# The last, short chunk of tokens goes through all experts densely instead of by scatter and gather

## The reference

```
x = h.reshape(T, D)                                  # T = 16 * 3137 tokens, D = 64
probs = softmax(x @ gate_w + gate_b); idx = argmax(probs); prb = probs[idx]
pos = (cumsum(one_hot) * one_hot).sum(-1) - 1        # place of the token in its expert's list
kept = pos < C                                       # C = ceil(1.25 * T / 8)
buf[idx, pos] = x
hmid = relu(buf @ w1 + b1)                           # 64 -> 256
ybuf = hmid @ w2 + b2                                # 256 -> 64
y_tok = ybuf[idx, min(pos, C - 1)] * (prb * kept)
h = h + y
```

## Time and profile before

| | |
|---|---|
| time, median of 3 runs | 4353.44 us (4352.43 to 4363.89) |
| the profiled execution's own time | 4361.58 us |
| its span, first to last instruction | 4359.7 us |
| PE busy | 3178.4 us (73%) |
| DVE busy | 2525.0 us (58%) |
| POOL busy | 2575.4 us (59%) |
| ACT busy | 2138.1 us (49%) |
| granted TensorE clock, mean | 0.863 of full |

### The profile page before, as it was taken

One profiled execution on the slowest core, in us unless ns is written; L12 is line 12 of the kernel. 1 busy time (PEld: TensorE's weight loads), 2 busy tenths in 40 slices (PEclk: granted clock), 3 DMA queues, 4 the chain that ended last, 5 costly groups with the idle time before them and its releaser, 6 DMA issues. The chain is left out here.

```text
span 4359.7 us, 68616 instructions
## 1 busy us (share of the span) xinstructions
PE 3178.4 (73%) x25552; PEld 1804.6 (41%) x25552; DVE 2525.0 (58%) x3049; ACT 2138.1 (49%) x3049; POOL 2575.4 (59%) x1541
## 2 busy tenths in 40 slices
PE   8999996999999940000099946676666899999997
PEld 6777774455555520000044312222221455555556
DVE  7888886888888851000055513333237777777772
ACT  6666665777777720000034335565552444444444
POOL 7777773878778716777600065555516666666661
PEclk9999998999999965555599967778777999999999
DMA  1111111122222121111133323333330111112111
GB/s 42 38 40 40 40 40 56 58 73 86 68 75 79 46 68 38 40 45 35 23 106 112 103 59 94 91 99 100 88 100 21 41 55 52 52 50 59 53 47 41
DMA packets 252194, 267.20 MB, mean 61 GB/s; under 512 B 86568, under 2 KB 168140, under 8 KB 251805
## 3 DMA queue, kind: packets, MB, share of 16 engines
q1 hardware_dynamic: 215566, 228.51, 16.8%
q0 software_dynamic: 25600, 21.10, 2.7%
q10 hardware_dynamic: 10704, 13.20, 0.9%
HBM read 127.66 MB, written 140.20 MB: 61 GB/s over the span
## 5 line engine op out<-in xcount | busy, mean ns | idle before, releaser
L1512 POOL DMA_INDIRECT D_row<-yb,D_idx x400 | 385.1, 963 | 635.8 <-DMA D_prob<-keepp 346.9
L2150 POOL TENSOR_TENSOR E_w<-E_w,E_rs 128x1024 f32<-128x1024 f32 x200 | 380.4, 1902 | 365.0 <-DVE E_rs L2073 365.0
L1241 POOL DMA_INDIRECT xb<-R_row,R_si x400 | 389.7, 974 | 212.2 <-issue 121.6
L1314 PE MATMUL X_px<-X_ident,X_xs 128*128 128x128 f32 x256 | 42.9, 291 | 559.6 <-DMA X_xs<-xb 559.6
L180 POOL TENSOR_TENSOR A_kmask<-A_ksb,A_pack_a 128x3584 f32<-128x3584 f32 x56 | 356.6, 6367 | 152.6 <-ACT A_ksb L327 152.6
L1373 ACT ACTIVATE X_hm<-X_ph,X_b 128x512 f32<-128x512 f32 x128 | 88.1, 688 | 595.6 <-PE X_ph L1326 595.6
L2058 DVE TENSOR_REDUCE E_mx<-E_lg 128x16 f32<-128x1024 f32 x200 | 244.9, 1224 | 219.6 <-PE E_lg L1867 219.3
L1388 DVE COPY X_xt<-X_px 128x512 f32<-128x512 f32 x64 | 43.6, 681 | 531.1 <-PE X_px L1314 531.1
L2144 POOL TENSOR_TENSOR E_hs<-E_w 128x512 f32<-128x512 f32 x200 | 255.1, 1275 | 93.4 <-ACT E_w L2031 93.4
L1879 PE MATMUL E_z<-E_w,E_yk 128*64 128x512 f32 (+1 forms) x800 | 224.5, 634 | 78.1 <-POOL E_w L2150 76.9
L1314 PEld LDWEIGHTS X_px<-X_ident,X_xs 128*128 128x128 f32 x256 | 27.5, 143 | 608.2 <-DMA X_b<-in_e_b 559.7
(11 more groups left out here) (292 smaller groups left out, 8394.0 us busy)
## 6 DMA issues: line engine op xcount, KB each, us to landing
xb<-B_blank SPq DMA_DIRECT2D x64, 256.0 KB, 3.9
X_xs<-xb SPq DMA_DIRECT2D x64, 256.0 KB, 2.8
yb<-X_ys SPq DMA_DIRECT2D x64, 256.0 KB, 2.0
B_x<-h SPq DMA_DIRECT2D x25, 512.0 KB, 4.2
h<-B_hh SPq DMA_DIRECT2D x25, 512.0 KB, 3.7
y<-B_yt SPq DMA_DIRECT2D x25, 512.0 KB, 2.6
R_row<-y SPq DMA_DIRECT2D x25, 512.0 KB, 3.3
A_xg<-in_xw SPq DMA_DIRECT2D x56, 224.0 KB
```

The costliest lines, as they stand in the source:

```text
L1241: pool.indirect_dma_start(out=xb, out_offset=bass.IndirectOffsetOnAxis(ap=si[:, B * c + b:B * c + b + 1], axis=0), in_=row[c % U][:, D * r ...
L1512: pool.indirect_dma_start(out=row[n % LR][:, k, b], out_offset=None, in_=yb, in_offset=bass.IndirectOffsetOnAxis(ap=idx[:, c, i:i + 1], ax ...
L2150: TT(w3, w3, bc(rs[g % 3][:].unsqueeze(2), [128, 2 * SH, G]), ALU.mult).then_inc(w_done, 1)
```

## The change

The last chunk leaves the scatter and the gather. Its 16 x 65 real tokens go through all eight experts in stage R, while POOL scatters the other 24 chunks. Two images lie on the two partition halves, and four pairs are side by side, so that a block has 4 x 65 = 260 columns; there are NB = 2 blocks and so 16 steps (block, expert). At each step the tokens of other experts are zeroed by a mask, and what eight experts make of a zero (their biases) is taken out again by a constant per chosen expert (`cbt`). All experts are added up in one PSUM accumulator, the sum is scaled by the probability and added to h1 in DRAM.

Stage D reads that sum from h1 for its narrow blocks and skips `weigh`, `turn_rows` and `add_experts` there. The narrow block's loaded buffer is read until `add_hidden`, and `load` waits for that.

The row buffers of R go from 6 to 4. The weights of X come in one packed transfer of 3418 values per partition, which R loads as well. Stage R has 26 more semaphores for the dense part and 4 fewer for the row buffers.

```diff
-def routing(nc, a, lg, y2, xb, gidx, keepp):
+def routing(nc, a, lg, y2, xb, gidx, keepp, h1):
-        N, U = CHUNKS * B, 6
+        N, U = CHUNKS * B, 4
...
                 sp.dma_start(flat(L)..., lg...).then_inc(loads_in, 16)
+                sp.dma_start(pack[:], a["pack_x"]).then_inc(w_in, 16)
+                sp.dma_start(pick[:], a["c_pick"]).then_inc(w_in, 16)
+                sp.dma_start(held[:], y2[LAST]).then_inc(held_in, 16)
...
# PE, beside the scatter
+                def mask(s):
+                    i, e = divmod(s, E)
+                    pe.wait_ge(ohc_done, i + 1)
+                    after(pe, xe_done, s - 1)
+                    mm(ob[s % 2], pick[:, 2 * D * e:2 * D * e + 2 * D], oht[i % 2], start=True, stop=True)...
+                def up(s):
+                    pe.wait_ge(xe_done, s + 1)
+                    for f in range(2):
...
+                        for b in range(2):
+                            last = mm(ph[b][f], w1[HALF[b], s % E, 128 * f:128 * f + 128], xe[s % 3][HALF[b], :], ...)
+                def down(s):
+                    for f in range(2):
...
+                        for b in range(2):
+                            last = mm(acc[HALF[b], :], w2[:, s % E, f], hm[s % 2][:, b, f], start=False, ...)
...
# DVE, before the scatter starts
                 TT(X[:], L[:], by(mx), ALU.subtract).then_inc(sub_done, 1)
+                dve.wait_ge(w_in, 32)
+                TS(rb1[:], part["b1"]..., 0.0, None, ALU.max).then_inc(rb_done, 1)
+                dve.wait_ge(rb_done, 1)
+                for f in range(2):
+                    last = TT(r8[:, :, f], ...)
                 dve.wait_ge(totc_done, len(cuts))
...
# DVE, beside the scatter
+                def masked(s):
...
+                    TT(xe[s % 3], ob[s % 2], xt[i % 2], ALU.mult).then_inc(xe_done, 1)
+                def relu(s, f, b):
...
+                    TS(hm[s % 2][:, b, f], ph[b][f], part["b1"][:, k:k + 1], 0.0, ALU.add, ALU.max)...
+                def final(i):
...
+                    TT(xo[i % 2], px, yt[i % 2], ALU.mult).then_inc(t_done, 1)
...
+                    TT(xo[i % 2], xo[i % 2], hx[i % 3], ALU.add).then_inc(xo_done, 1)
...
# POOL
-                for c in range(CHUNKS):
+                for c in range(LAST):
...
 def experts(nc, a, xb, yb):
-                    spread(nc, sp, loads[:-1], consts)
+                sp.dma_start(pack[:], a["pack_x"]).then_inc(consts, 16)
...
 def image_recurrence(...):
+        Z = PAIRS * (J - 1)
+        def sparse(n):
+            return n % J != J - 1
+        def before(n):
+            if n >= N:
+                return Z
+            return n // J * (J - 1) + n % J
...
                 def load(n):
-                    after(sp, x_done, n - LH + 1)
+                    if n >= LH:
+                        if sparse(n - LH):
+                            sp.wait_ge(x_done, before(n - LH) + 1)
+                        else:
+                            sp.wait_ge(h_done, n - LH + 1)
...
-                for n in range(N):
-                    after(pool, sc_done, n - LR + 1)
+                for z in range(Z):
+                    after(pool, sc_done, z - LR + 1)
+                    n = block_of(z)
...
                 def turn_rows(n):
+                    if not sparse(n):
+                        return
...
                 def center_in(n):
-                    pe.wait_ge(x_done, n + 1)
+                    token_ready(pe, n)
...
                 def turn_y(n):
                     pe.wait_ge(yo_done, n + 1)
-                    after(pe, x_done, min(n + 5, N))
+                    after(pe, x_done, before(n + 5))
+                    after(pe, yk_done, n)
...
                 def weigh(n):
+                    if not sparse(n):
+                        return
...
                 def add_experts(n):
+                    if not sparse(n):
+                        return
```

More of the change, by code:

```diff
@@ L25 @@
 BLK = 512
+DENSE_PAIRS = 4
 CAPP = -(-CAP // BLK) * BLK
@@ L43 @@
     "f": (("ident", 128), ("bo", 1)),
+    "x": (("w1", E * F), ("w2", 2 * E * D), ("b1", 2 * E), ("b2t", E), ("ident", 128), ("other", 2 * E * E), ("b2r", D),
+          ("half", 2)),
 }
@@ new lines, in _, with turn_x @@
+                pe.wait_ge(w_in, 32)
+                pe.wait_ge(r8_done, 1)
+                for e in range(E):
+                    for f in range(2):
+                        last = mm(acc[0:2 * E, 0:D], r8[:, e, f], w2[:, e, f], start=e + f == 0, stop=e + f == E)
+                last.then_inc(c_done, 1)
+                pe.wait_ge(totc_done, len(cuts))
+                pe.wait_ge(prb_done, 1)
+                def turn_x(i):
+                    pe.wait_ge(held_in, 16)
+                    after(pe, t_done, i - 1)
+                    for k in range(BT):
+                        for b in range(2):
+                            r = D * row_of(2 * (BT * i + k) + b)
+                            last = mm(px[HALF[b], tokens(k)], held[0:TAIL, r:r + D], ident[0:TAIL, 0:TAIL],
+                                      start=True, stop=True)
+                    last.then_inc(turn_done, 1)
@@ new lines, in turn_oh @@
+                def turn_oh(i):
+                    pe.wait_ge(xtc_done, i + 1)
+                    for k in range(BT):
+                        last = turn(px[0:2 * E, tokens(k)], oh[0:TAIL, images(i, k)].rearrange("p b e -> p (b e)"),
+                                    ident[0:TAIL, 0:TAIL])
+                    last.then_inc(oht_done, 1)
+                def mask(s):
+                    i, e = divmod(s, E)
+                    pe.wait_ge(ohc_done, i + 1)
+                    after(pe, xe_done, s - 1)
+                    mm(ob[s % 2], pick[:, 2 * D * e:2 * D * e + 2 * D], oht[i % 2], start=True, stop=True).then_inc(mask_done, 1)
@@ new lines, in prob @@
+                def prob(i):
+                    pe.wait_ge(ohc_done, min(i + 2, NB))
+                    after(pe, t_done, i)
+                    for k in range(BT):
+                        n = images(i, k).start
+                        for b in range(2):
+                            last = mm(px[HALF[b], tokens(k)], bc(prb[0:TAIL, n + b:n + b + 1], [TAIL, D]),
+                                      ident[0:TAIL, 0:TAIL], start=True, stop=True)
+                    last.then_inc(pb_done, 1)
@@ new lines, in bias @@
+                def bias(i):
+                    pe.wait_ge(ohc_done, i + 1)
+                    pe.wait_ge(cbt_done, 1)
+                    after(pe, yt_done, i)
+                    mm(acc, cbt[:].rearrange("p b d -> p (b d)"), oht[i % 2], start=True, stop=False, skip_group_check=True)
+                def down(s):
+                    for f in range(2):
+                        pe.wait_ge(relu_a, by_act(s, f))
+                        pe.wait_ge(relu_v, by_dve(s, f))
+                        for b in range(2):
+                            last = mm(acc[HALF[b], :], w2[:, s % E, f], hm[s % 2][:, b, f], start=False,
+                                      stop=s % E == E - 1 and f == 1, skip_group_check=True)
+                    last.then_inc(down_done, 1)
@@ new lines, in _ @@
+                turn_x(0)
+                turn_oh(0)
+                mask(0)
+                mask(1)
+                for s in range(S + 1):
+                    i, e = divmod(s, E)
+                    if s < S:
+                        up(s)
+                    if s + 2 < S:
+                        mask(s + 2)
+                    if e == 2 and i + 1 < NB:
+                        turn_x(i + 1)
+                    if e == 4 and i + 1 < NB:
+                        turn_oh(i + 1)
+                    if e == 6:
+                        prob(i)
+                    if s >= 1:
+                        if (s - 1) % E == 0:
+                            bias((s - 1) // E)
+                        down(s - 1)
@@ L1272, in experts @@
         yv = yb.rearrange("(n p s) d -> n p (s d)", p=128, s=8)
[L1273 to L1278, removed]
+        CN = 16
         with nc.Block() as block:
```

213 lines of the change are left out of this document (181 added, 32 removed).

## The result

The changed kernel took 4397.98 us (4394.4 to 4402.9, 5 runs) against 4353.44 (4347.4 to 4363.9, 5 runs): ratio 1.0095, 95% interval 1.0076 to 1.0114. I had forecast 4336.

A forecast was written before the change was run, and what follows sets the result against it. Bounds: POOL's scatters in R, the joint turn of DVE, PE and ACT in D, PE in X. Sum -20.5 + 1.6 + 0.5 - 2.5 + 7.6 - 4 = -17.3 us, so 4336 us; own range 4327 to 4365, with rivals 4316 to 4357.

The forecast's parts named there:

- Dense work: Stage R: 16 steps at 9.6 us, 154 us, hidden in 491 us of scatter that leave PE, DVE, ACT idle; cost nothing.
- rival 4: Stage R: the dense work is not hidden; it would have to take over 491 us; chance 0.02.
- slower by over 0.3%: Whole kernel: outcome slower than before by more than 0.3% (13 us); chance 0.08, with 0.28 for within it.
- Even three times that much would just fit: Stage R: three times the dense work's estimated 154 us would still fit beside 491 us of scatter.
- Scatter, -20.5: Stage R: 16 of 400 scatters removed at 1.28 us each on POOL, the only busy engine: -20.5 us.
- DVE slowing POOL, 0: Stage R: DVE's dense instructions might lengthen POOL's scatters by 0 to 21.2 us; taken as 0.
- R's opening, +2.1: Start of stage R: 22 more semaphores cleared, +1.6 us; constants delayed by SP's weight load, +0.5 us.
- X's opening, -2.5: Start of stage X: one packed weight load shortens the 12.2 us to the first matmul by 0.5 to 3.4; taken -2.5 us.
- Narrow turns and gathers saved in D, 0: Stage D: DVE skips three steps in 8 turns, but ACT is late next, and gathers don't set the pace; no gain.
- SP's blocked queue, +7.6: Stage D: narrow block's load waits for `add_hidden`, holding back the stores behind it; `tokens` late in seven places, +7.6 us.
- PE's stalls, -4: Stage D: PE's late results come by number of gathers; 16 fewer save one stall of 0 to 7.2 us; taken -4.

The follow-up runs named there:

- experiment 1: Changed kernel without the dense steps themselves, all else of the change kept: 4330.27 us, 0.9939 of before, where before takes 4353 to 4356 us.
- experiment 2: Kernel before plus idle work beside its 400 scatters (DVE products, ACT copies, PE matmuls): 4387.45 us, where before takes 4353 to 4356 us.
- experiment 7: Two kernels rerun unaltered on the second kind of chip: the changed one, 4179.24 us (0.9991 of before), and that of experiment 2, 4182.06 us.
- 5: Kernel before with the idle work of experiment 2, POOL's 400 transfers plain, without index list: 3872.1 us, on a chip where before takes 4176.5 us.
- 8: The plain-transfer kernel of 5 run again unaltered, three times, on the second kind of chip: 3885.6, 3874.7 and 3889.7 us.
- experiment 4: Changed kernel with the second of its two dense blocks left out: 4348.53 us, on a chip where the kernel before takes 4353 to 4356 us.

## Why the prediction was wrong

**Dense work, "I cost it at nothing": the step that failed.** Its price came from stage X, where POOL issues nothing: 9.6 us a step at most. Beside the scatter, on a chip of the first kind, a pass costs 2.6 to 2.8 us whatever its width, so a step of 18 passes takes some 50 us, and 198 of the 364 passes fit beside it after the quick ones at the start. 128 passes were left for behind the scatter. Where the price is absent, behind the scatter or on the second kind, a step takes 2.7 us, far below the 9.6: the estimate failed by the price alone. This is rival 4, to which I gave 0.02 (and which I then left out of the chances: slower by over 0.3% should have read 0.10, within it 0.26); it cost +39 us up to X's first issue, where -18.4 was forecast. "Even three times that much would just fit" was no margin: 364 passes at 2.8 us are 1019 us, more than six times 154. The warning was in the rows. The prediction counted stalls of PE in stage D that come with POOL's gathers and end with them, and said that no row shows what makes them. It priced them for D and never asked what they would do to work moved next to 384 transfers in a row. That they are the same thing is likely, not shown: on the second kind, where no link or pass is long, the kernel before is some 175 us shorter, and stage D is 178 us shorter (555.2 us, in the kernel before with idle work in R, against 733.3), while the scatter, with that idle work beside it, takes 512.5 us against 510.4.

**Scatter, -20.5:** right where the dense steps are absent (experiment 1) or quick (489.6 us on the second kind). With them on the first kind it is +1.0.

**DVE slowing POOL, 0:** right. On the second kind 384 scatters beside all dense work are 0.972 us in the median. A chain of products with both inputs in SBUF does lengthen the indirect scatters beside it, on both kinds: 1.08 us and 1.39 from start to start between 1660 and 1680 (experiments 2 and 7). The plain transfers of 5 and 8, which have no list of indices, take 0.54 us beside the same chain as behind it.

**R's opening, +2.1:** the clears were right, the transfer was not. The stage's first DVE instruction in the kernel before and in the changed one:

```profile
1581.65 0.39 DVE L1181 MEMSET R_onesr<- 128x400 f32 x1 [5.12 <-PEq L82]
```
```profile
1581.58 0.39 DVE L1381 MEMSET R_onesr<- 128x400 f32 x1 [6.83 <-PEq L85]
```

DVE waits 1.7 us longer for the opening, where +1.6 was forecast. From SP's first issue to the first scatter it is then 66.3 us instead of 67.2, where +0.5 was forecast. Ten traces of the change lie within 0.4 us of this.

**X's opening, -2.5:** -4.7 (12.2 to 7.5 us; 12.5 to 7.6 on the second kind). The 1.75 MB come faster than the 313 GB/s that I had as the better bound: 359 GB/s from 2149 to 2153 in experiment 7. And one gain that I had not seen: from the last scatter to SP's first issue 9.2 us instead of 13.2 (experiments 1 and 7). POOL waits for four semaphores instead of six at the end, but that is not it: its drain of the block starts 2.4 us after the last scatter's start as against 2.3 before, and then takes 5.28 us instead of 9.20, in six traces of the change against five with the six buffers. What shortens it is open.

**Narrow turns and gathers saved in D, 0:** right, as far as single traces tell. On the second kind a pair takes 64.3 us on average with five buffers and 65.4 in the kernel before, with 48 gathers instead of 50.

**SP's blocked queue, +7.6:** right in place and kind, too small. It is +17.3 on the second kind in the pair of traces shown: 5.5 us up to the first pair's end, 8.4 over the six pairs between, 3.4 in the last. Stage D takes 570.5 to 580.9 us in four traces of the change there and 546.7 to 561.3 in seven with the stage D of before, 21 us apart on average; with five buffers it takes 556.2 and 555.8. `tokens` starts 3.8 us after the narrow sum's end, where I took 3.4; but I had set against it what `tokens` waits anyway on the first kind (up to 4.2 us), and on the second kind that cover is 1.6 in each pair: 7 x 2.2 = 15.4. On the first kind `tokens` comes 3.6 to 5.0 us after the sum's end in the changed kernel, but the stage as a whole shows nothing of it: 719.6 to 733.7 us in four traces of the change, 733.3 and 723.4 in two of before.

**PE's stalls, -4:** not to be read there, for the same scatter.

On the second kind the two profiled executions add up: -29.8 to X's first matmul, +17.3 in D, in all -12.6 (spans 4167.6 and 4180.2). The medians show only -3.7; the profiled execution of the change is the shortest of its ten, and where the others are longer is not known.

## What to carry to other kernels

Before you call idle engines beside POOL's transfers free, find a stretch of the same trace in which they work beside such transfers, and take the price there: per instruction, not per column. A stall "that no row explains" is a price until it is explained; ask what it would cost the work that you move next to its likely source. When a buffer gets a later last reader, look for the load that refills it and for what stands behind that load in its queue; here two more buffers took the kernel from 0.9991 to 0.9942 of before, on the second kind.

## What the runs showed of the hardware

- On one kind of chip, beside POOL's indirect scatters, chains on ACT and PE fall to 1.40 us per instruction after 9 to 14 us of normal speed, in steps of 0.70 us. In the changed kernel passes are bunched at times, and then a pause of 2.8 us for each pass of the step before follows. Normal speed is back at 2186, 27 us after the last scatter's start. On four other chips, all traced later, nothing of it. The granted clock doesn't explain it: it is 0.50 from 1668 to 2184, and also from 1645 to 1668 in the same trace, where the passes are quick.
- On that kind of chip the slowness outlasts the work: POOL's semaphore clears in experiment 4 still come late, mostly by steps of 0.7 us, until 2181, 24 us after the last scatter ended (2157.4), and in experiment 2 the scatters have 1.40 us from start to start after the other engines have finished.
- What takes the 0.70 us was not shown. Each execution timed here was also recorded, so the recording itself can't be excluded. The Trainium skill (page "NOTIFIC — the notification-queue block", section "7.1 Overflow: three behaviours, one of which stalls the engine") says that the path on which trace records leave can hold an engine back when it fills. Two records per instruction, each waiting 0.70 us, would look like what the rows show; no run here was made without records, so this is a candidate and no more. If it is the cause, a time on a chip of the first kind holds a share that the kernel itself doesn't need.
- A chain of DVE products of 128x260 with both inputs in SBUF takes 0.46 us a link beside POOL's scatters and 0.75 beside POOL copies of 128x512 (two traces, second kind). The other way round it lengthens an indirect scatter from 0.97 to 1.08 us (both kinds) and a plain transfer (0.54 us) not at all (four traces, second kind).
